# V from the transposed context, weighted sums in 64x64 tiles and the output matrix, in place of context mixes and merged matrices

## The reference

```python
ln = layernorm(x)
q, k, v = ln @ Wq, ctx @ Wk, ctx @ Wv              # 16 heads of 64
attn = softmax(causal(q @ k.T / 8))                # per sequence and head, 56 x 56
x = x + tanh(g_xattn) * (concat_h(attn @ v) @ Wo)
h = rmsnorm(layernorm(x)) * gamma1                 # the second block, per row
q = h @ Wq2 + bq ; k, v = (h @ Wdown + bdown) @ Wup + bup    # 16 heads of 8
o = softmax_over_heads(q @ k.T / sqrt(8)) @ v      # 16 x 16 for each row
y = layernorm(x) + (o @ Wo2 + bo)
h2 = rmsnorm(y) * gamma2 ; gate = softmax(h2 @ Wg + bg)      # 8 experts
out = x + tanh(g_ffn) * (y + sum_e gate_e * (h2 @ We_e))
```

## Time and profile before

| | us |
|---|---|
| median of 3 runs (283.01 to 329.11) | 283.18 |
| the profiled execution | 282.62 |
| its span in the trace | 280.7 |
| TensorE busy | 248.0 |
| VectorE busy | 209.7 |
| ScalarE busy | 159.8 |
| GpSimd busy | 153.5 |

### The profile page before, as it was taken

One profiled execution on the slowest core, in us unless ns is written; L12 is line 12 of the kernel. 1 busy time (PEld: TensorE's weight loads), 2 busy tenths in 40 slices (PEclk: granted clock), 3 DMA queues, 4 the chain that ended last, 5 costly groups with the idle time before them and its releaser, 6 DMA issues.

```text
span 280.7 us, 6097 instructions
## 1 busy us (share of the span) xinstructions
PE 248.0 (88%) x2350; PEld 184.3 (66%) x2350; DVE 209.7 (75%) x370; ACT 159.8 (57%) x432; POOL 153.5 (55%) x189
## 2 busy tenths in 40 slices
PE   7989899998999999999999999999999796852660
PEld 6776589685969695959595959585968374621220
DVE  0266623599989898989897429999998979998500
ACT  2536424554686858576767575657677364633431
POOL 4104032335468585758585554545859476759444
PEclk9999999999999999999999999999999799996665
DMA  6995000000000000000000000000000000000000
GB/s 213 352 349 227 0 4 0 2 1 2 2 0 12 0 13 0 13 1 12 0 12 2 9 2 9 4 2 1 11 0 2 11 2 9 1 9 0 12 9 9
DMA packets 7483, 9.28 MB, mean 33 GB/s; under 512 B 542, under 2 KB 5919, under 8 KB 7327
## 3 DMA queue, kind: packets, MB, share of 16 engines
q1 hardware_dynamic: 7022, 8.25, 9.0%
q10 hardware_dynamic: 432, 0.64, 0.6%
HBM read 7.97 MB, written 0.92 MB: 32 GB/s over the span
## 4 chain that ended last, share of the span: by engine, by line
PE 73%; DVE 8%; POOL 7%; ACT 6%; issue 5%; POOLq 0%; ACTq 0%; DVEq 0%
PE ps_a L681 37%; PE ps_b L681 13%; PE ps_c L681 11%; PE ps_b L723 4%; PE ps_e L681 4%; POOL exb L294 2%; ACT zT L372 2%; DVE prod L560 1%; DVE ps_e L546 1%; PE ps_b L678 1%; POOL probs L265 1%; ACT exb L427 1%; ACT probsT L386 1%; POOL exb L296 1%; DVE prod L537 1%
## 5 line engine op out<-in xcount | busy, mean ns | idle before, releaser
L681 PE MATMUL ps_a<-zT,m_sb 128*128 128x112 f32 x512 | 62.5, 276 | 1.6 <-ACT zT L372 1.1
L681 PEld LDWEIGHTS ps_a<-zT,m_sb 128*128 128x128 f32 x512 | 60.1, 192 | 3.1 <-ACT zT L372 1.3
L265 POOL TENSOR_TENSOR probs<-probs,prinv 120x672 f32<-120x672 f32 x16 | 24.3, 1517 | 41.5 <-DVE prinv L510 41.5
L274 POOL TENSOR_TENSOR prod<-fqkv 128x768 f32<-128x768 f32 x14 | 25.4, 1816 | 23.4 <-DVE fqkv L532 23.4
L427 ACT ACTIVATE exb<-ps_c,gate 128x128 f32<-128x128 f32 x112 | 32.3, 383 | 7.0 <-PE ps_c L681 5.5
L681 PE MATMUL ps_c<-fwe_sb,x2T 128*128 128x512 f32 x56 | 31.9, 699 | 4.9 <-DVE glog L587 4.9
L379 ACT ACTIVATE probs<-ps_b,rstd 120x896 f32<-120x896 f32 x15 | 15.1, 1007 | 34.0 <-PE ps_b L681 34.0
L546 DVE TENSOR_REDUCE ps_e<-prod 128x256 f32<-128x2048 f32 x14 | 32.0, 2285 | 0.1
L571 DVE TENSOR_REDUCE oraw<-prod 128x128 f32<-128x2048 f32 x14 | 31.2, 2227 | 0.0
L537 DVE TENSOR_TENSOR prod<-ps_e,fqkv 128x1280 f32<-128x1280 f32 x14 | 20.9, 1492 | 11.2 <-ACT ps_e L398 11.2
L294 POOL TENSOR_TENSOR exb<-exb 128x640 f32<-128x640 f32 x14 | 21.6, 1539 | 13.1 <-ACT exb L427 13.0
(11 more groups left out here) (124 smaller groups left out, 448.7 us busy)
## 6 DMA issues: line engine op xcount, KB each, us to landing
ctx_sb<-in_ctx SPq DMA_DIRECT2D x1, 1024.0 KB, 10.4
xp_sb<-in_xp SPq DMA_DIRECT2D x1, 896.0 KB, 9.6
out<-out_sb SPq DMA_DIRECT2D x14, 64.0 KB, 1.5
xT<-in_x_t SPq DMA_DIRECT2D x1, 784.0 KB, 6.2
cT<-in_ctx_t SPq DMA_DIRECT2D x1, 784.0 KB, 8.2
wvt_sb<-in_wv_t SPq DMA_DIRECT2D x1, 512.0 KB, 7.8
wo_sb<-in_wo SPq DMA_DIRECT2D x1, 512.0 KB, 9.0
ctx_sb<-in_ctx SPq DMA_DIRECT2D x2, 256.0 KB, 9.8
```

Of the source, the lines that this page charges most:

```text
L265: nc.gpsimd.tensor_tensor(pr[0:TG, NC:C, :, 0:S], pr[0:TG, NC:C, :, 0:S], prinv[p % 2][0:TG, NC:C, :].unsqueeze(3).to_broadcast([TG, C - N ...
L274: nc.gpsimd.tensor_tensor(prod1[:, 0:HP, :, :], t[:, D:2 * D].rearrange("p (g d) -> p g d", g=FH).unsqueeze(1).to_broadcast([128, HP, FH, ...
L681: return nc.tensor.matmul(o, lhsT, rhs, start=start, stop=stop, skip_group_check=True)
```

## The change

V is now made for each pair: values multiplies the transposed context cT (64 columns of a sequence, of which 56 count) by wv_sb, 512 columns for each of two column halves of TensorE, into one bank, and ScalarE copies the bank. attend multiplies V by the turned probabilities, 32 products of 64x64 tiles, two sequences by 16 heads, into both banks of ps_a; ScalarE's attended copies each. new_y then needs eight products with wo_sb, whose head order in chunks 4 to 7 is swapped on the host. The merged matrices, the context in rows (2 MB of loads), zT and the z semaphores go. The hiding term is written as four products of 64x64 tiles. The scores wait for the copies of the turned probabilities of the pair two steps of the bank before in place of the z copies. HP is 8 and HQ is 5. The slots are in another order on each engine. Waits and names that follow from this alone are left out below.

```diff
-HP = 6
-HQ = 3
+HP = 8
+HQ = 5
...
+    fills("k", 0, range(4))
+    fills("q", 0, range(4))
+    fills("v", 0, range(2))
+    fills("q", 1, range(4))
+    fills("v", 1, range(2))
+    fills("k", 1, range(4))
+    fills("o", 0, range(2))
+    new_y(0)
+    fills("o", 1, range(2))
+    for t in range(2, NP + 1):
+        new_y(t - 1)
         for kind, g, k in PROJECT_AT.get(t, ()):
-            projections(kind, g, (k,))
+            fills(kind, g, (k,))
         if t < NP:
-            mixes(t)
+            fills("v", t, range(2))
+            fills("o", t, range(2))
     return uses
...
-            sp.dma_start(wvt_sb[:, :, :], wv_t.rearrange("(c p) d -> p c d", c=C)).then_inc(s["wvt_in"], 16)
+            sp.dma_start(wv_sb[:, :, :], wv.rearrange("d (r n) -> d r n", r=2)).then_inc(s["wv_in"], 16)
+            sp.dma_start(xT[:, GT:], x_t[:, GT:]).then_inc(s["xT_in"], 16)
+            sp.dma_start(cT[:, GT + G - S:], ctx_t[:, GT + G - S:]).then_inc(s["cT_in"], 16)
             sp.dma_start(wo_sb[:, :, :], wo.rearrange("(c p) f -> p c f", c=C)).then_inc(s["wo_in"], 16)
-            sp.dma_start(ctx_sb[:, 0:4, :], ctx2[:, 0:4, :]).then_inc(s["ctx0_in"], 16)
-            sp.dma_start(xT[:, GT:], x_t[:, GT:]).then_inc(s["xT_in"], 16)
-            sp.dma_start(cT[:, GT:], ctx_t[:, GT:]).then_inc(s["cT_in"], 16)
             sp.dma_start(fw_sb[:, :], fw).then_inc(s["fw_in"], 16)
             sp.dma_start(fup_sb[0:L + 1, :], fup).then_inc(s["fup_in"], 16)
             sp.dma_start(fdn_sb[0:L, :], fdn).then_inc(s["fdn_in"], 16)
             sp.dma_start(xp_sb[:, 2:NP, :], xp[:, 2:NP, :]).then_inc(s["xp_in"], 16)
             sp.dma_start(fwe_sb[:, :, :], fwe.rearrange("e d f -> d e f")).then_inc(s["fwe_in"], 16)
-            sp.dma_start(ctx_sb[:, 4:8, :], ctx2[:, 4:8, :]).then_inc(s["ctx1_in"], 16)
-            sp.dma_start(ctx_sb[:, 8:16, :], ctx2[:, 8:16, :]).then_inc(s["ctx2_in"], 16)
-            sp.dma_start(ctx_sb[:, 16:32, :], ctx2[:, 16:32, :]).then_inc(s["ctx3_in"], 16)
...
+                if fc is not None:
+                    residual(fc)
                 if fb is not None:
                     products(fb)
-                if fc is not None:
-                    residual(fc)
                 if fd is not None:
                     outputs(fd)
+                if t < NP:
+                    norm(t)
                 if fc is not None:
                     second_scale(fc)
-                if t < NP:
-                    norm(t)
+                if fa is not None:
+                    first_scale(fa)
                 if fb is not None:
                     weighted(fb)
                 if fc is not None:
                     gating(fc)
-                if fa is not None:
-                    first_scale(fa)
...
-            def mixed(p, bt):
-                for r in range(2):
-                    if bt == 0:
-                        act.wait_ge(a_full[r], USES["z", p, r][1])
-                    else:
-                        act.wait_ge(z_full[r], p + 1)
-                    nc.scalar.copy(zT[p % 2][:, :, r, bt * S:(bt + 1) * S],
-                                   (score_banks(p) if bt else ps_a)[:, r, 0:C * S].rearrange("p (c q) -> p c q", c=C)
-                                   ).then_inc((z_free if bt else a_free)[r], 1)
+            def values(p, bt):
+                b, n, _ = USES["v", p, bt]
+                act.wait_ge(a_full[b], n)
+                nc.scalar.copy(v_sb[p % 2][:, bt, :, :], ps_a[:, b, :].rearrange("p (c d) -> p c d", c=C)).then_inc(a_free[b], 1)
+
+            def attended(p, half):
+                b, n, _ = USES["o", p, half]
+                act.wait_ge(a_full[b], n)
+                nc.scalar.copy(aT[p % 2][:, 4 * half:4 * half + 4, :],
+                               ps_a[:, b, 0:4 * T].rearrange("p (c t) -> p c t", c=4)).then_inc(a_free[b], 1)
...
             nc.scalar.copy(wqc[:, 0:4, :], ps_e[:, 0, :].rearrange("p (c f) -> p c f", c=4)).then_inc(s["wqc_copied_act"], 1)
             for k in range(4):
                 project("q", 0, k)
+            values(0, 0)
+            values(0, 1)
             exps(0)
             exps(1)
             act.wait_ge(s["fw_in"], 16)
             nc.scalar.activation(gates[:, :], fw_sb[:, COL_GATES:COL_GATES + 2], ACT.Tanh).then_inc(s["gates_ready"], 1)
             for k in range(4):
                 project("q", 1, k)
+            values(1, 0)
+            values(1, 1)
             turned_probs(0)
-            mixed(0, 0)
+            for k in range(4):
+                project("k", 1, k)
             turned_probs(1)
-            mixed(0, 1)
-            project("k", 1, 0)
-            project("k", 1, 1)
-            mixed(1, 0)
-            project("k", 1, 2)
-            project("k", 1, 3)
-            mixed(1, 1)
+            attended(0, 0)
+            attended(0, 1)
+            attended(1, 0)
+            attended(1, 1)
...
+                for fill in PROJECT_AT.get(t, ()):
+                    project(*fill)
                 if fc is not None:
                     squares(fc)
+                if fa is not None:
+                    x1_copy(fa)
+                if fc is not None:
+                    x2_copy(fc)
+                if t < NP:
+                    values(t, 0)
                 if fb is not None:
                     head_exps(fb)
                 if fc is not None:
-                    x2_copy(fc)
-                for fill in PROJECT_AT.get(t, ()):
-                    project(*fill)
-                if fa is not None:
-                    x1_copy(fa)
-                if fc is not None:
                     gate_exps(fc)
                 if t < NP:
+                    values(t, 1)
                     turned_probs(t)
-                if fc is not None:
-                    experts(fc, 0)
-                if t < NP:
-                    mixed(t, 1)
                 if fa is not None:
                     kv_copy(fa)
                 if t < NP:
-                    mixed(t, 0)
-                if fc is not None:
+                    attended(t, 0)
+                    attended(t, 1)
+                if fc is not None:
+                    experts(fc, 0)
                     experts(fc, 1)
...
+                if t < NP:
+                    score_max(t)
+                if t <= NP:
+                    new_x1(t - 1)
                 if fb is not None:
                     products(fb)
-                if t < NP:
-                    score_max(t)
-                if fb is not None:
-                    logits(fb)
                 if fc is not None:
                     new_x2(fc)
-                if fb is not None:
-                    shifted_logits(fb)
-                if t <= NP:
-                    new_x1(t - 1)
                 if t < NP:
                     prob_sums(t)
                     norm(t)
                 if fb is not None:
-                    weighted(fb)
+                    logits(fb)
+                if fa is not None:
+                    tile_stats(fa)
+                if fb is not None:
+                    shifted_logits(fb)
                 if fc is not None:
                     gate_logits(fc)
                 if fa is not None:
-                    tile_stats(fa)
+                    scaled_qkv(fa)
                 if fc is not None:
                     gate_sum(fc)
                 if fb is not None:
+                    weighted(fb)
                     mixed_heads(fb)
-                if fa is not None:
-                    scaled_qkv(fa)
-                if fb is not None:
                     normed_heads(fb)
...
+            def values(p, bt):
+                b, n, ys = USES["v", p, bt]
+                free_bank(b, n, ys)
+                t0 = (2 * p + bt) * S
+                for r in range(2):
+                    ins = mm(ps_a[r * G:(r + 1) * G, b, :], cT[:, t0:t0 + G], wv_sb[:, r, :])
+                ins.then_inc(a_full[b], 1)
+
             def scores(p):
                 banks, q, k, t0 = score_banks(p), qT[p // 2 % 2], kT, p % 2 * T
-                for r in range(2):
-                    if p >= 2:
-                        pe.wait_ge(z_free[r], p)
+                if p >= 2:
+                    last = p if p > 2 else 1
+                    pe.wait_ge(s["pT_lo"], last)
+                    pe.wait_ge(s["pT_hi"], last)
+                for bt, r in ((0, 0), (1, 1), (1, 0), (0, 1)):
                     rows = slice(r * G, r * G + S)
-                    mm(banks[0:TG, r, 0:C * S], both_b[rows, :, :].rearrange("p b q -> p (b q)")[:, 0:TG],
+                    mm(banks[bt * G:(bt + 1) * G, r, 0:C * S], ident_b[rows, r * G:(r + 1) * G],
                        hide_b[rows, :, :].rearrange("p c k -> p (c k)"), stop=False)
...
-            def mix(p, bt):
-                pe.wait_ge(s["pT_ready"], 2 * p + 2)
-                for r in range(2):
-                    if bt == 0:
-                        free_bank(*USES["z", p, r])
```

(89 more changed lines are left out.)

82 lines of the change are left out of this document (25 added, 57 removed).

## The result

Changed kernel: 279.66 us, median of 16 runs; kernel before, beside it: 283.06 (16 runs). Ratio 0.9865, 95% interval 0.9836 to 0.9893: 1.35% faster, and less than the 2% that counts as a difference. The forecast was 268. The profiled execution took 278.05 us with a span of 276.1, where 265.8 was forecast.

The account below looks back on a forecast made before the run. TensorE was taken to set the pace (14.50 busy of a 14.53 us step), VectorE close behind. Span: 280.7 - 8.1 (steps) - 3.5 (before the loop) - 3.3 (end) = 265.8; 268 as median, range 261 to 273, chance 0.60.

Parts of the forecast that it names:

- The sign: Whole kernel: faster than before with chance 0.78, same 0.12, slower 0.10.
- TensorE in a full step: TensorE's work in a full step falls from 14.53 to 13.67 us: mixes, half of new_y go; values, attend come.
- the two rivals that priced those, at 288 and 275: Values' column halves in series: 288, chance 0.20. Attend two tiles at a time: 275, sharing 0.20 with the third rival.
- The rule of the Trainium skill on row tiles and banks: Attend: different row tiles cannot use one PSUM bank at once; if binding, attend takes 1.5 instead of 1.05 us.
- VectorE in a full step: Moving heads to GpSimd saves VectorE 0.26 us each in products and weighted; its step falls to 13.3 with gaps.
- GpSimd pays 1.2 in all, hidden: GpSimd in a full step: 0.6 us more each for products and weighted; uncovered, up to 1.2 us cost.
- The loop through ScalarE: Longest loop, shift to next shift through ScalarE, VectorE and TensorE: 13.95 us; step taken as 14.0 against 14.53.
- the third rival: ScalarE's loop stays 14.5 as experts' copies hold up exps: 276; chance 0.20 shared with attend two tiles at a time.
- All steps: Gain over the loop's steps: 8.1 us together, of which 3.6 in steps 4 to 8.
- The expected loss of clock in step 14: Step 14: TensorE, with less to do, runs partly at its lower 1.2 GHz level; gain only 0.9 us.
- Before the loop: Ahead of the loop: combined matrices, mixes and half of new_y(0) go, values and attends come; gain 3.5 us.
- The end: Last steps: step 16 from 11.85 to about 10.6, gain 1; earlier gate logits in step 17, gain 2.3; together 3.3 us.

Follow-up runs that it names:

- e6: e1 with 32 tiny products behind the warm-up, shifting all that follows in TensorE's stream by 64 load-product pairs; 280.62 us, ratio 0.9908.
- e7: e1 with 16 tiny products behind the warm-up, shifting TensorE's stream by 32 load-product pairs; 282.12 us, ratio 0.9961.
- e13: e1 with attend between the two expert halves and the turning of the probabilities ahead of values; 287.2 us, ratio 1.0147.
- e2: Changed kernel with GpSimd's products put ahead of its residual, onorm unchanged; 276.38 us, ratio 0.9763.
- e3: Changed kernel with HP, the heads of products on GpSimd, at 6 instead of 8; 278.21 us, ratio 0.9824.
- e1: Changed kernel with VectorE's weighted sums written to PSUM, so that onorm has one SBUF input; 276.35 us, ratio 0.9773 to the kernel before.
- e8: e1 with the heads split as before the change (HP = 6, HQ = 3); 278.95 us, ratio 0.9845.
- e11: Changed kernel's new mathematics and head split, with the slots of all four engines in the order of the kernel before; 294.76 us, ratio 1.0437.

## Why the prediction was wrong

The sign and most of the prices were right. The span came out 10.3 us over the forecast, and three steps of the working failed: the sum of TensorE's busy times was taken as the step (4.4 us of halts), GpSimd's added work was called hidden (2.6), and a wait at the end was counted as part of a step and not on top of it (2.0). The other 1.3 are small: 0.8 ahead of step 2 and 0.5 in the steps.

- **TensorE in a full step: right, then wrong.** The sum 13.67 measured 13.90. The two column halves of values do run together (1.87 for the pair; 3.46 was the other end), attend is 1.08 with both row tiles of a half in one bank, so the two rivals that priced those, at 288 and 275, are out. Of its pieces new_y took more (2.04, not 1.77) and the values (1.87, not 1.73), the hiding term with the scores less (1.02, not 1.31). The rule of the Trainium skill on row tiles and banks that was weighed there (TensorEngine Tiling (Array Packing), Restrictions and Gotchas) would give 1.5 for attend; 1.08 says that it doesn't bind in this layout. What failed is that a sum of busy times was taken as the step: it has no term for the supply of instructions, and values and attend raised TensorE's products, as the profile counts them, from 2350 to 3118 and put 132 short ones in a row. Missed: 4.4 us in this profile, the largest of the three. That the halts go by the place in the stream is shown by e6 and e7, that they need the dense run by e13; no variant that leaves nothing out got the time back.
- **VectorE in a full step: "hidden" failed.** "GpSimd pays 1.2 in all, hidden" looked at GpSimd's own time only. Its products start ahead of onorm, since fqkv is now made ahead of weighted, and end behind its start, since they are longer by two heads and stand behind residual. Without the place behind residual (e2) onorm is free; with two heads less (e3) it is held 0.14 us and not 0.63; the place of fqkv was not tested by itself. Cost 2.6 us, shown twice (e1, e2), but mostly outside the full steps that this part of the prediction was about: 0.3 in steps 4 to 8, 1.0 in steps 9 to 15, 1.3 behind them. The 0.26 saved in products and weighted are there, and e8 shows them worth nothing in a full step.
- **The loop through ScalarE: the number right, by luck.** 13.95 forecast; 13.94 measured in e1, where neither theory's cost is in the step. But the chain of that step is TensorE's work alone, 13.90 of it: the step is TensorE's sum, 0.23 over its forecast. The loop is shown to be no longer than that, not to be 13.95. The experts' copies, at their end at 96.1 in e1, did not hold up exps at 97.9, so the third rival is out too.
- **All steps.** 8.1 forecast. e1 without its halts has 25.3 + 70.3 + 97.2 = 192.8 for steps 2 to 15, against 200.4 before: 7.6 gained. The halt-free part was priced well in the sum. The expected loss of clock in step 14 came, with the experts at 3.6 us.
- **Before the loop.** Forecast 3.5, gained 2.7 (3.1 in e1). The 0.4 between these two lie ahead of the first scores, which begin at 14.65 and 14.21; from there to step 2 both take 22.75, where the kernel before took 25.66.
- **The end: 3.3 forecast, nothing gained, and 1.3 in e1.** Between starts of VectorE's products steps 16 and 17 gained what was said and more, in e1 from 11.85 to 10.49 and from 7.41 to 4.67 (to glog). But the stretch begins with step 16's own products, and these stand behind new_x1, hence behind new_y and the copy of attend. They began 0.6 us behind the last mix before and begin 3.4 behind the last attend now (234.79 to 238.16). I had that wait in the 10.6 of step 16, as a part; it comes on top. onorm adds 1.35 in step 17, where it took 1.65.

Together: 10.3 = 4.4 of halts + 2.6 of exclusion + 2.0 at the end + 0.8 before the loop + 0.5 in the steps. Without halts e1's span is 3.0 us under the changed kernel's (2.4 between the spans, and 0.6 of longer halts in e1); 0.4 of that lie before the loop, where onorm does not run yet, and 2.6 are the exclusion. The other 2.0 and 0.5, and 0.4 of the 0.8, are what e1 without halts lacks against the forecast. That products wait at the end is read from the trace; no variant tested it.

The experiments also correct the attribution. The change reads as new mathematics with a tidied order, and the forecast got its gain from the mathematics. e11 shows that the order carries 15 us: without it the same mathematics is 4% slower than the kernel before. Which of the moved slots matter most was not taken apart; e11's chain points to kv_copy; and the traces of before, e2 and e11 suggest that the new places of scaled_qkv and residual together let the exclusion in.
